# Filler products on TensorE in and ahead of the first attention, and one activation table set for logarithm and exponential

## The reference

```python
x = x + tanh(g_xattn[0]) * L0_xattn(layernorm(x), ctx, ...)   # stage A
x = x + tanh(g_ffn[0])   * L0_ffn(layernorm(x), ...)          # stage B
x = x + tanh(g_xattn[1]) * L1_xattn(layernorm(x), ctx, ...)   # stage C
x = x + tanh(g_ffn[1])   * L1_ffn(layernorm(x), ...)          # stage D
```

```python
q = _ln((x @ Wq + bq).reshape(b, s1, H, HD), qn_w, qn_b)      # 16 heads of 16, normalised per head
k = _ln(kv[..., :HD], kn_w, kn_b);  v = kv[..., HD:]          # from the context, 128 features
ctx = _attn(q, k, v) + _attn(q, k_dca, v_dca)                 # 48 keys, and 16 keys with weights of their own
return ctx @ Wo + bo
```

## Time and profile before

| what | us |
|---|---|
| median of three runs | 490.94 |
| lowest and highest | 490.15 and 494.52 |
| the profiled execution, its time | 492.26 |
| the profiled execution, its span from first to last instruction | 490.2 |

### The profile page before, as it was taken

How to read it: one execution, slowest core, us unless ns; L and a number is a source line. 1 busy time by engine, 2 the same in 40 slices (tenths; PEclk the granted TensorE clock), 3 DMA queues, 4 the chain that set the end, 5 groups by cost and what they waited for, 6 DMA issues and landing times. The chain is left out here.

```text
span 490.2 us, 7799 instructions
## 1 busy us (share of the span) xinstructions
PE 413.8 (84%) x2996; PEld 389.4 (79%) x3004; DVE 341.2 (70%) x754; ACT 205.8 (42%) x405; POOL 163.4 (33%) x194
## 2 busy tenths in 40 slices
PE   0637794958666899999999899999999999879996
PEld 0536783857555898999999889999999999869995
DVE  4775759587530576768586488988989978956652
ACT  3263536535222143433433356446455555413331
POOL 3013322142230022222313154464464464334332
PEclk9958596795955599999999999999999999979999
DMA  8103001010010003011020200100100100000000
GB/s 254 40 1 114 16 9 58 0 64 2 28 79 1 0 1 109 1 61 49 15 94 1 67 2 1 57 0 1 57 2 1 46 1 1 1 2 23 23 19 25
DMA packets 6648, 16.25 MB, mean 33 GB/s; under 512 B 1090, under 2 KB 4291, under 8 KB 6100
## 3 DMA queue, kind: packets, MB, share of 16 engines
q1 hardware_dynamic: 6612, 15.75, 9.7%
HBM read 14.70 MB, written 1.05 MB: 32 GB/s over the span
## 5 line engine op out<-in xcount | busy, mean ns | idle before, releaser
L1421 POOL TENSOR_SCALAR work<-work,lut_step,lut 128x344 f32<-128x344 int32 (+1 forms) x60 | 42.1, 712 | 55.3 <-DVE work L1348 53.7
L291 PE MATMUL ps<-wB_hi,workr 128*128 128x256 f32 x224 | 52.6, 298 | 6.0 <-POOL workr L1576 4.5
L291 PE MATMUL ps<-xT_hi,wB_hi 128*128 128x256 f32 x176 | 53.0, 301 | 0.0
L291 PE MATMUL ps<-xT_lo,wB_hi 128*128 128x256 f32 x176 | 51.3, 291 | 0.0
L291 PE MATMUL ps<-xT_hi,wB_lo 128*128 128x256 f32 x176 | 51.2, 291 | 0.0
L291 PE MATMUL ps<-wN_hi,shared_r 128*128 128x256 f32 x256 | 47.5, 280 | 1.3 <-DVE x L1335 1.3
L1014 POOL TENSOR_TENSOR workr<-work,workr 128x256 fp32r<-128x256 f32 (+1 forms) x36 | 22.9, 636 | 71.3 <-ACT workr L897 71.3
L291 PEld LDWEIGHTS ps<-wB_hi,workr 128*128 128x128 f32 x224 | 39.4, 194 | 8.0 <-POOL wB_lo L1426 3.8
L1363 DVE COPY_PREDICATED work<-work 128x1376 f32<-128x1376 int32 (+5 forms) x36 | 41.3, 1146 | 2.3
L291 PEld LDWEIGHTS ps<-wN_hi,shared_r 128*128 128x128 f32 x256 | 40.1, 188 | 1.5 <-DVE shared_r L1325 1.5
L291 PE MATMUL ps<-xT_hi,wM_hi 128*128 128x256 f32 x128 | 36.7, 287 | 3.2 <-ACT work L1189 1.6
(11 more groups left out here) (199 smaller groups left out, 1188.6 us busy)
## 6 DMA issues: line engine op xcount, KB each, us to landing
stage<-in_wC SPq DMA_DIRECT2D x4, 1280.0 KB, 5.4
stage<-in_wB SPq DMA_DIRECT2D x4, 768.0 KB, 4.4
stage<-in_idx SPq DMA_DIRECT2D x4, 536.0 KB, 3.6
stage<-in_wA SPq DMA_DIRECT2D x2, 512.0 KB, 5.6
out<-x SPq DMA_DIRECT2D x4, 256.0 KB, 2.2
x<-in_x SPq DMA_DIRECT2D x1, 768.0 KB, 6.9
ctx_T<-in_ctx_T SPq DMA_DIRECT2D x1, 512.0 KB, 8.0
ctx_n<-in_ctx_n SPq DMA_DIRECT2D x4, 128.0 KB, 2.2
```

The source lines that it names most:

```text
L291: last = nc.tensor.matmul(out, l, r, start=start and i == 0, stop=stop and i == 2)
L1421: nc.gpsimd.tensor_scalar(lev[:, j, 0:n], bits[:, 0, 0:n], lut_step[:, j:j + 1], lut[:, 2 * j:2 * j + 1], ALU.mult, ALU.add).then_inc(*C[" ...
```

## The change

- A helper issues n products of a 128x128 piece of the split weights with 512 columns of the same into a PSUM bank that is written again before it is read. It stands in nine places of stage A: ahead of the first transposes (10 products), behind the queries of group 0 (22), behind its transposes of queries and keys (10); then in every group behind the shift (14), behind the first transposes of probabilities (4), ahead of the second product with the values (3); in the last group behind that product (6); in the last two groups ahead of the product with Wo (5) and at the group's end (9).
- PE begins when the upper part of the first half of the weights is there, and waits for the lower parts behind the first transposes.
- The DMA of the gates moves from the twelfth place of SP's queue to the fifth, ahead of the context. ACT takes the tanh of the gates before `act_A_start` and then loads the table set `natural_log_exp_and_others` by name. DVE waits for the tanh once, ahead of group 0.

```diff
+        def keep_warm(n, bank):
+            for _ in range(n):
+                nc.tensor.matmul(ps[:, bank, :], shared_r[:, 0:P], shared_r[:, 0:512], start=True, stop=True)
+
         def pe_A_start(pe):
+            pe.wait_ge(wA_hi_ready, 1)
+            keep_warm(10, 0)
             front_pe(pe, 0, 7)
+            pe.wait_ge(wA_lo_ready, 2)
             pe_A_kv(pe, 0)
             pe_A_q(pe, 0)
+            keep_warm(22, 0)
             front_pe(pe, 1, 7)
             pe_A_turn(pe, 0)
+            keep_warm(10, 0)
             for t in range(TILES):
                 pe_A_scores(pe, 0, t)
             pe_A_kv(pe, 1)
...
             pe_A_shift(pe, g, 0)
             pe_A_shift(pe, g, 1)
+            keep_warm(14, 7)
             pe_A_probs(pe, g, 0)
+            keep_warm(4, 7)
             if more:
                 pe.wait_ge(*A["q_ready"].at(n, 1))
             pe_A_values(pe, g, 0)
...
             pe_A_probs(pe, g, 1)
             if more:
                 front_pe(pe, g + 2, 1)
+            keep_warm(3, 7)
             pe.wait_ge(*A["x_done"].at(g, 0))
             pe_A_values(pe, g, 1)
+            if not more:
+                keep_warm(6, 4)
...
             pe_A_turn_out(pe, g)
             if two_more:
                 pe_A_kv(pe, g + 2)
+            else:
+                keep_warm(5, 4)
             pe_A_out(pe, g)
             if more:
                 pe_A_scores(pe, n, 1)
+            if not two_more:
+                keep_warm(9, 4)
...
             sp.dma_start(const, a["const"]).then_inc(const_in, 16)
+            sp.dma_start(gates, a["gates"].partition_broadcast(P)).then_inc(gates_in, 16)
             sp.dma_start(ctx_T, a["ctx_T"]).then_inc(ctxT_in, 16)
...
             sp.dma_start(x[:, TILES:, :], xr[:, TILES:, :]).then_inc(x_in, 16)
-            sp.dma_start(gates, a["gates"].partition_broadcast(P)).then_inc(gates_in, 16)
...
             pe.wait_ge(const_in, 16)
-            pe.wait_ge(wA_lo_ready, 2)
             pe_A_start(pe)
...
             act.wait_ge(setup_pool, 4)
+            act.wait_ge(gates_in, 16)
+            nc.scalar.activation(tg, gates, ACT.Tanh).then_inc(tg_ready, 1)
+            nc.scalar.preload_act_table_set("natural_log_exp_and_others")
             act_A_start(act)
-            act.wait_ge(gates_in, 16)
-            nc.scalar.activation(tg, gates, ACT.Tanh).then_inc(setup_act, 1)
...
             dve_A_start(dve)
+            dve.wait_ge(tg_ready, 1)
```

More of the change, by code:

```diff
@@ L211, in build @@
         A_prep_in = sem("A_prep_in")
-        ident_A_ready = sem("ident_A_ready")
+        ident_A_ready, tg_ready = sem("ident_A_ready"), sem("tg_ready")
         padded = sem("padded")
```

## The result

The changed kernel takes **471.59 us** (median of 4 runs, 471.19 to 472.73), the kernel before 491.56 beside it (4 runs, 490.15 to 494.52): a ratio of 0.959, with a 95% interval of 0.9541 to 0.9639. Its profiled execution took 471.44 us, with a span of 469.5 and a mean granted clock of 0.992, where before it was 492.26, 490.2 and 0.906. Where executions of one kernel lay over 1.5% above its fastest (three of ten in e1_table_only, one of four in e6_seven), the ratios leave these slow ones out, while medians and ranges hold all.

The account below looks back on a forecast made before the run. Stage A was taken as a chain through five engines with TensorE at 1.2 GHz for long stretches. 3.9 + 6.9 + 6.5 - 0.5 + 2.9 = 19.7 us off gave 472 us, range 467.5 to 481.

Parts of the forecast that it names:

- The opening: Stage A up to the first scores: fillers raise the clock, 3.9 us saved, between 2.5 and 4.8.
- The first term: Ten fillers ahead of the first key and value products: VectorE's waits of 1.27 us shrink, less 0.2 delay, 1.0 saved.
- The turn: Eight transposes of group 0's queries and keys: 1.97 us to about 1.1, half of the 0.87 counted, 0.4.
- Groups 0 to 2: Stage A's first three groups: faster transposes and value products, earlier POOL; 2.3 us each, 6.9 in all, between 4.5 and 8.
- The last group: End of stage A, no other group's work in its chain: 6.5 us saved, between 5 and 7.
- Stage B's first group: Its first products at full clock bring the first tanh and routing weights earlier: 2.9 us saved.
- the step that failed: Stage B's first tanh: its table load of 1.28 us was claimed hidden in ACT's 11.05 us of idle time.
- The rest: Stages C and D, not touched by the change: clock falls and rises there worth 1 to 2 us either way.
- Rival 1: Stage A: transposes and 64-column products let the clock fall; in part 476 to 481, chance 0.14; in full 485, 0.06.
- Rival 2: Stage A's fillers all run at 1.2 GHz and overrun their pauses by 20 us: 511, chance 0.02.
- Rival 3: Stage B: tanh's table set lacks the exponential, two loads of 1.28 us in each of four groups: 482, chance 0.03.
- Rival 4: Opening and last group as forecast, but fillers in groups 0 to 2 run at 1.2 GHz: 487, chance 0.02.

Follow-up runs that it names:

- e1_table_only: Kernel before with only the table set change, tanh ahead, and no fillers; 492.48 us, ratio 0.9975 to the kernel before.
- e6_seven: Changed kernel with 7 fillers in place of the 14 in each softmax pause; 475.06 us, ratio 0.9623 to the kernel before.
- e8_tuned: Changed kernel with 31 fillers for 22, four more ahead of the turn, eight for nine, and tanh's table set loaded by name ahead of stage B; 470.08 us.
- e2_fill_only: Changed kernel with all fillers, but gates' DMA, tanh and table loads as in the kernel before; 474.74 us, ratio 0.9684 to the kernel before.
- e10_no_tail: Changed kernel without the six fillers of the last group and the five and nine of each of the last two groups; 475.31 us.
- e3_exp_set_back: Changed kernel with the set of exponential and tanh loaded by name behind ScalarE's last instruction of stage A; 471.68 us.
- e9_no_opening: Changed kernel without the opening's 42 fillers and with the opening's old order; 475.06 us, ratio 0.9631 to the kernel before.
- e4_no_14: Changed kernel without the 14 fillers of each softmax pause; 477.75 us, ratio 0.976 to the kernel before.
- e5_turns: Changed kernel with 32 transposes of the identity in place of the 14 fillers in each softmax pause; 471.73 us, ratio 0.9602 to the kernel before.
- e7_28: Changed kernel with 28 fillers in place of the 14 in each softmax pause; 480.16 us, ratio 0.977 to the kernel before.
- e12_tuned_and_D: e8_tuned with 14 more fillers in TensorE's pause in stage D; 467.74 us, ratio 0.9522 to the kernel before.

## Why the prediction was right

The time (472.0 forecast, 471.59 measured) and the account behind it held; one step of it was wrong, one was half wrong, and two terms were too careful. In part they offset each other: the span shrank by 20.7 us, where the sum had 19.7.

**The opening**, 3.9 forecast, 3.4 measured. The first term is exact in sum (1.0, seen at the queries' add), though the ten fillers made the first transposes 0.46 late (13.74) and not 0.2. The opening of one and the same code varies by about as much, so this agreement is in part luck. The scores gave 2.3 where I had 2.5. The turn gave nothing where I had put half of its 0.87: the 22 fillers stop 4.5 us before it, and the clock fell. e8_tuned, which closes that gap, got the 0.85. The moved DMA and the load of the table set ahead of the context's casts cost nothing, as costed.

**Groups 0 to 2**, 2.3 each forecast, 2.7 measured, 8.1 in all instead of 6.9. Each step of the walk is to be seen in the rows: 0.9 at the first transposes, 1.7 at the product with the values, and POOL's end as the next late event. Two terms were mis-sized. The table set gave 0.8, not 0.7 (e2_fill_only), and the three fillers, which I had 0.25 late, were some 0.1 late: ScalarE's copy ends at 83.23 in the second group and the product that needs it starts at 83.38. That "only if the clock is up" the set counts was shown by e1_table_only, where it is worth nothing.

**The last group**, 6.5 less 0.5 for the nine, so 6.0 forecast and 6.56 measured. The nine were some 0.2 late: the first product of B starts 0.40 us behind the end of the update of x (143.63), 0.22 before. That they are "the price of entering stage B warm" is right in direction; e10_no_tail, which doesn't pay it, loses 0.9 in B.

**Stage B's first group**, 2.9 forecast, 2.76 measured, and here **the step that failed** is "ACT is idle for 11.05 us ahead of that tanh, so it is hidden". A pause long enough is not a load that stands in it. The load came when the wait was over and put 1.28 us ahead of the tanh, and 0.67 us into the stage, as e2_fill_only and e3_exp_set_back show alike. It is not seen in the total because a second step was off the other way.
**The rest** moved by 0.07 us between these two profiled executions. That is luck: from the first cast of B's second group to the end it took 301.5 us in e8_tuned and 306.9 in e9_no_opening, with the same instructions; the clock stood at 0.50 for none of it in the one and for 10.2 us in the other. So the 1 to 2 us that I gave it were too few.

**The rivals.** Rival 1, that thin work doesn't hold the clock, fell with the windows of the result (1.00 through every group); e4_no_14 shows what such falls cost where the later fillers stay, 5 to 6 us, and e5_turns that transposes hold the clock too. Rival 2 fell with the prices: the first ten fillers ran at 1.2 GHz, and the twelve products behind them mostly at 2.4; of the rest only the ten ahead of the scores began at 0.50, and took 3.41 us in place of 2.5. Its mechanism is real, though: e7_28 overran every pause and lost 8.6 us of the 20. Rival 3 fell with ScalarE's rows in stage B, where one load stands and none in the groups after: the set that holds tanh serves the exponential too. Rival 4 needed what rival 2 needed, and fell with it.

## What to carry to other kernels

Where the granted clock falls in a pause on a chain, look at how long what stands behind the pause takes at both levels; products or transposes that nobody reads, ending a little ahead of the releaser, buy the difference, and too many of them cost what they overrun. Place the fillers up to the point where the next work starts, not where the last one ends: 22 that stopped 4.5 us short gave nothing to the turn. Fill the shorter pauses ahead of the long one too: without them, 14 fillers started at the lower clock (e10_no_tail). Before a table set is merged or a wait is taken away, find what is next late at the present clock, and load the set that the next stage needs by name in the pause ahead of it.

## What the runs showed of the hardware unexpectedly

A table load that the program does not place can stand on either side of a wait. In stage B it began behind ScalarE's wait for PE (147.04, after 7.46 us idle). In the groups of the kernel before, the first load of a group ran ahead of the wait of the logarithm behind it:

```profile
48.69 1.28 ACT L389 ACT_TABLE_LOAD   x1
50.19 0.26 ACT L389 ACTIVATE workA<-workA 128x64 f32<-128x64 f32 x1 [0.21 <-DVE workA L426]
```

It began 0.02 us behind ScalarE's previous instruction, and the logarithm then waited for VectorE. One difference can be seen: ahead of stage B's first tanh the program has two waits in a row, and the trace has one of them as an instruction of its own (EVENT_SEMAPHORE, L908, at 147.0), with the load behind it; at L389 there is one wait and no such instruction. That this decides was not tried. Placed by name the load took the same 1.28 us and was hidden.

Two identical openings (e9_no_opening and e1_table_only) lay 1.1 us apart at the first shift, by the moments at which the clock rose. From the first cast of B's second group on (the last 2 us aside), the two profiled executions in which the clock never fell took 301.2 and 301.5 us (e12_tuned_and_D, e8_tuned); the twelve others, with 3.4 to 10.2 us of it at 0.50, took 302.6 to 306.9. With the clock held nearly everywhere (e12_tuned_and_D, 0.998 and more) the six runs spread by 2.65 us all the same, so the clock is not all of it. What the rest is was not looked for.
